# Three rounded products in place of two full-precision ones for the attended rows of the second attention block

## The reference, cut to what matters

```python
def _L1_xattn_ref(text, features, Wq, bq, Wk, bk):
    Q = jnp.einsum('btx,dx->btd', text, Wq) + bq
    K = jnp.einsum('bpx,dx->bpd', features, Wk) + bk
    scores = jnp.einsum('btd,bpd->btp', Q, K) * scale
    attn = jax.nn.softmax(scores, axis=-1)
    attended = jnp.einsum('btp,bpd->btd', attn, features)
    return attended
...
x = x + _L1_xattn_ref(_layernorm(x, axis=-1), ctx_4096, L1_xattn_Wq, L1_xattn_bq, L1_xattn_Wk, L1_xattn_bk)
```

## Time and profile before

| | |
|---|---|
| median of 3 runs | 2158.94 us (2157.11 to 2161.94) |
| the profiled execution, its own time | 2155.61 us |
| its span from the first to the last instruction | 2153.8 us |
| busy: TensorE / weight loads | 2119.5 us (98%) / 1667.0 us (77%) |
| busy: VectorE / ScalarE / GpSimd | 1854.2 us (86%) / 1155.1 us (54%) / 260.4 us (12%) |

### The profile page before, as it was taken

One profiled execution on the slowest core, in us unless ns is written; L12 is line 12 of the kernel. 1 busy time (PEld: TensorE's weight loads), 2 busy tenths in 40 slices (PEclk: granted clock), 3 DMA queues, 4 the chain that ended last, 5 costly groups with the idle time before them and its releaser, 6 DMA issues.

```text
span 2153.8 us, 35686 instructions
## 1 busy us (share of the span) xinstructions
PE 2119.5 (98%) x11487; PEld 1667.0 (77%) x11487; DVE 1854.2 (86%) x3099; ACT 1155.1 (54%) x1722; POOL 260.4 (12%) x302
## 2 busy tenths in 40 slices
PE   9979999999999999999999999999999999999998
PEld 7857777778777777787777778777777787777776
DVE  8268898988888998888898988888998888898984
ACT  4145555655555565555555655555565555555652
POOL 0001111111101110111111111101110111111100
PEclk9999999999999999999999999999999999999999
DMA  6354343333343323334343333343323334343310
GB/s 217 142 156 127 118 132 102 95 119 126 127 134 119 117 90 105 127 127 136 117 130 103 95 119 125 128 134 120 117 89 106 127 127 136 117 129 104 93 54 30
DMA packets 110874, 254.03 MB, mean 118 GB/s; under 512 B 12976, under 2 KB 14272, under 8 KB 110848
## 3 DMA queue, kind: packets, MB, share of 16 engines
q1 hardware_dynamic: 110848, 253.69, 36.3%
HBM read 215.89 MB, written 20.97 MB: 110 GB/s over the span
## 4 chain that ended last, share of the span: by engine, by line
PE 84%; DVE 6%; issue 3%; ACT 1%; DVEq 0%; POOL 0%; POOLq 0%; ACTq 0%
PE acc L1192 17%; PE shared L1121 7%; PE shared L1166 6%; PE shared L1167 6%; PE scores L1181 5%; PE scores L1180 5%; PE acc L1152 4%; PE scores L1141 4%; PE acc L1155 4%; PE acc L1153 4%; PE shared L1357 3%; PE shared L1284 3%; PE scores L1127 2%; PE scores L1307 2%; DVE neg_max L880 2%
## 5 line engine op out<-in xcount | busy, mean ns | idle before, releaser
L991 DVE TENSOR_TENSOR p_lo<-prob,p_hi 128x1024 fp32r<-128x1024 f32 x256 | 312.2, 1219 | 103.6 <-ACT p_hi L790 85.7
L783 ACT ACTIVATE prob<-scores 128x1024 f32<-128x1024 f32 x256 | 260.8, 1019 | 241.1 <-PE scores L1181 189.9
L880 DVE TENSOR_REDUCE neg_max<-scores 128x1 f32<-128x1024 f32 x256 | 309.4, 1220 | 44.8 <-PE scores L1141 42.1
L696 POOL TENSOR_TENSOR rstd<-var_eps,minus_half 128x1 f32<-128x1 f32 x128 | 126.2, 986 | 1746.1 <-DVE var_eps L870 1746.1
L790 ACT ACTIVATE p_hi<-prob 128x1024 fp32r<-128x1024 f32 x256 | 271.3, 1060 | 42.7 <-PE acc L1192 38.5
L1152 PE MATMUL acc<-m_hi,cT_hi 128*128 128x512 f32 x512 | 218.3, 426 | 3.6 <-DVE cT_lo L1052 2.7
L1166 PE MATMUL shared<-signT,y_hi 128*128 128x512 f32 x512 | 205.5, 401 | 0.0
L1155 PE MATMUL acc<-m_ring,cT_hi 128*128 128x512 f32 x512 | 203.3, 397 | 0.0
L1153 PE MATMUL acc<-m_hi,cT_lo 128*128 128x512 f32 x512 | 203.1, 397 | 0.0
L1180 PE MATMUL scores<-q_hl,k_hh 128*128 128x512 f32 x512 | 201.0, 392 | 1.8 <-DVE q_m L973 1.4
L1181 PE MATMUL scores<-q_m,k_l 128*128 128x512 f32 x512 | 202.0, 395 | 0.0
(11 more groups left out here) (219 smaller groups left out, 4201.5 us busy)
## 6 DMA issues: line engine op xcount, KB each, us to landing
m_ring<-m_low SPq DMA_DIRECT2D x512, 256.0 KB, 3.2
c_in<-in_ctx SPq DMA_DIRECT2D x32, 512.0 KB, 3.3
xn<-in_x SPq DMA_DIRECT2D x32, 512.0 KB, 4.2
x<-in_x SPq DMA_DIRECT2D x32, 512.0 KB, 3.2
c_val<-in_ctx SPq DMA_DIRECT2D x32, 512.0 KB, 3.7
out_x<-oscale SPq DMA_DIRECT2D x32, 512.0 KB, 3.0
q_m<-q_hl SPq DMA_DIRECT2D x32, 256.0 KB, 3.1
k_hh<-k_hh SPq DMA_DIRECT2D x32, 256.0 KB, 3.5
```

The lines of the kernel that those rows point to most:

```text
L783: nc.scalar.activation(prob[s % 2][:, :], scores[s % 2][:, :], ACT.Exp).then_inc(exp_ready, 1)
L880: nc.vector.tensor_reduce(neg_max[:, t:t + 1], scores[t % 2][:, :], AX_X, ALU.max, negate=True).then_inc(row_max, 1)
L991: nc.vector.tensor_tensor(p_lo[s % 2][:, :], prob[s % 2][:, :], p_hi[s % 2][:, :].bitcast(F32), ALU.subtract).then_inc(p_lo_ready, 1)
```

## The change

The context rows are split into a rounded part `val_hi` (a copy on ScalarE, after `p_hi` of step 4) and a remainder `val_lo = c_val - val_hi` (a subtraction on GpSimd, between `norm_scale(0)` and `norm_scale(3)`). The turned weights are split into `attnT_hi` (the copy on ScalarE that was `attnT`, now rounded) and `attnT_lo` (a subtraction on VectorE, behind the reciprocal of step 6). TensorE makes three products for each half instead of one. It waits for `attnT_lo` and `val_lo` ahead of the first. `val_hi` lies in the memory of `oscale`, `val_lo` in that of `c_val` and `attnT_lo` in that of `attn`.

```diff
--- before.py
+++ after.py
@@ -484,8 +484,12 @@
 
         xnT = sb("xnT", [P, T, P])
         den_wide = xnT[:, 0:2, :].rearrange("p t c -> p (t c)")
-        oscale = sb("oscale", [P, D])
-        c_val = sb("c_val", [P, D])
+        with ExitStack() as before:
+            oscale = sb("oscale", [P, D], F32, before)
+        val_hi = sb("val_hi", [P, D], F32R)
+        with ExitStack() as before:
+            c_val = sb("c_val", [P, D], F32, before)
+        val_lo = sb("val_lo", [P, D], F32R)
         stat = [sb(f"stat{i}", [P, 12]) for i in range(4)]
         mean_var = [sb(f"mean_var{i}", [P, 2]) for i in range(4)]
         neg_mean = [sb(f"neg_mean{i}", [P, 1]) for i in range(4)]
@@ -506,9 +510,11 @@
         xn_1 = xn_3 = p_sum
         xn_2 = oscale
         result = oscale
-        attn = sb("attn", [P, P])
+        with ExitStack() as before:
+            attn = sb("attn", [P, P], F32, before)
+        attnT_lo = sb("attnT_lo", [P, P], F32R)
         gate_parts = attn
-        attnT = sb("attnT", [P, P])
+        attnT_hi = sb("attnT_hi", [P, P], F32R)
         low = attn
         lowT_hi = sb("lowT_hi", [P, P], F32R)
         lowT_lo = sb("lowT_lo", [P, P], F32R)
@@ -596,6 +602,9 @@
         s_max_ready = sem("s_max_ready")
         attn_ready = sem("attn_ready")
         attnT_ready = sem("attnT_ready")
+        attnT_lo_ready = sem("attnT_lo_ready")
+        val_hi_ready = sem("val_hi_ready")
+        val_lo_ready = sem("val_lo_ready")
         x3_ready = sem("x3_ready")
         l_max_ready = sem("l_max_ready")
         l_exp_ready = sem("l_exp_ready")
@@ -707,6 +716,10 @@
                         norm_scale(2, c)
                     if prepare:
                         norm_scale(0, b)
+                    if chain:
+                        pool.wait_ge(val_hi_ready, nth(1, c, 1))
+                        pool.wait_ge(key_col_ready, nth(1, c, 1))
+                        nc.gpsimd.tensor_tensor(val_lo[:, :], c_val[:, :], val_hi[:, :].bitcast(F32), ALU.subtract).then_inc(val_lo_ready, 1)
                     if chain:
                         norm_scale(3, c)
                     if attend:
@@ -791,6 +804,10 @@
                         if chain and s == 3:
                             act.wait_ge(x2_ready, nth(2, c, 2))
                             normalize(2, c, xn_2, res)
+                        if chain and s == 4:
+                            act.wait_ge(val_loaded, nth(16, c, 16))
+                            act.wait_ge(xnT_done[2], nth(2, c, 2))
+                            nc.scalar.activation(val_hi[:, :], c_val[:, :], ACT.Identity).then_inc(val_hi_ready, 1)
                         if chain and s == 6:
 
                             act_chain.begin(c)
@@ -805,7 +822,7 @@
                         if chain and s == 6:
                             act.wait_ge(attnT_done, nth(1, c, 1))
                             act.wait_ge(att_done, nth(2, c - 1, 2))
-                            nc.scalar.activation(attnT[:, :], shared[1][:, 0:P], ACT.Identity).then_inc(attnT_ready, 1)
+                            nc.scalar.activation(attnT_hi[:, :], shared[1][:, 0:P], ACT.Identity).then_inc(attnT_ready, 1)
                     if prepare:
                         for h in range(2):
                             act.wait_ge(qk_done, nth(2, b, h + 1))
@@ -1024,6 +1041,9 @@
                         if chain and s == 6:
                             dve.wait_ge(attn_ready, nth(1, c, 1))
                             dve_chain.chain(dve, nc.vector.reciprocal(r_inv[1][:, :], r_sum[1][:, :]))
+                            dve.wait_ge(attnT_ready, nth(1, c, 1))
+                            nc.vector.tensor_tensor(attnT_lo[:, :], shared[1][:, 0:P], attnT_hi[:, :].bitcast(F32),
+                                                    ALU.subtract).then_inc(attnT_lo_ready, 1)
                     if chain:
 
                         for h in (1, 0):
@@ -1296,10 +1316,14 @@
                             transposes(0, kw, kwT_done)
                         if chain and s == 7:
                             pe.wait_ge(attnT_ready, nth(1, c, 1))
-                            pe.wait_ge(val_loaded, nth(16, c, 16))
-                            mm(shared[1][:, :], attnT[:, :], c_val[:, half(1)], start=True, stop=True).then_inc(att_done, 1)
-                            pe.wait_ge(kwT_ready, nth(2, a, 2))
-                            mm(shared[0][:, :], attnT[:, :], c_val[:, half(0)], start=True, stop=True).then_inc(att_done, 1)
+                            pe.wait_ge(attnT_lo_ready, nth(1, c, 1))
+                            pe.wait_ge(val_lo_ready, nth(1, c, 1))
+                            for h in (1, 0):
+                                if h == 0:
+                                    pe.wait_ge(kwT_ready, nth(2, a, 2))
+                                mm(shared[h][:, :], attnT_hi[:, :], val_hi[:, half(h)], start=True, stop=False)
+                                mm(shared[h][:, :], attnT_hi[:, :], val_lo[:, half(h)], start=False, stop=False)
+                                mm(shared[h][:, :], attnT_lo[:, :], val_hi[:, half(h)], start=False, stop=True).then_inc(att_done, 1)
                         if prepare and s == 7:
                             pe.wait_ge(c_loaded, nth(16, b, 16))
                             pe.wait_ge(exp_ready, nth(8, a, 7))
```

## The result

| | before | after |
|---|---|---|
| median | 2158.03 us (2154.97 to 2161.94) | 2214.05 us (2213.0 to 2214.69) |
| ratio | | 1.0256, 95% interval 1.0243 to 1.0269 |
| span of the profiled execution | 2153.8 us | 2212.8 us |

The change makes the kernel 56 us slower. A turn has become 1.83 us longer (62.14 to 63.96 us, from one start of the block's projections to the next, mean of twenty turns), and 31 times 1.83 is 56.7.

The account below looks back on a forecast made before the run. TensorE was taken to bound the whole, with VectorE without slack in the walk. Per turn 0.61 - 0.32 + 1.77 = 2.06 us, times 31 is 63.9; with 2155.6 and 3.3 that gave 2222 us, range 2178 to 2243.

Parts of the forecast that it names:

- its first rival: In the walk, GpSimd is held and VectorE keeps going; products start 2.4 us late, 2.08 a turn, 2223 us; chance 0.12.
- Sharing in pieces: GpSimd and VectorE slow each other; VectorE loses some 0.3 to 1.2 us a turn, 2177 to 2205 us; chance 0.10.
- The hold: At step 5, VectorE's p_lo waits for the end of GpSimd's val_lo: 1.77 us late, bounds 0 and 2.40.
- attnT_lo, 0.61 us late: At the attended rows, attnT_lo behind VectorE's reciprocal lets the first product start at 1097.05 instead of 1096.44: 0.61 us late.
- The saving of 0.32 us: At the attended rows, six rounded products replace two of full precision on TensorE: 0.32 us less per block.
- The sum per turn: Over one turn, late attnT_lo less TensorE's saving plus VectorE's wait: 0.61 - 0.32 + 1.77 = 2.06 us.
- val_hi free: ScalarE's copy of 1.06 us in the walk costs nothing, covered by 1.51 us of idle time, about 0.45 left.
- the fifth case: Faster: VectorE isn't held, TensorE's 0.61 us come back later in the turn, 10 us saved, 2149 us; chance 0.05.

Follow-up runs that it names:

- the run with both repairs: Changed kernel with the context rows split before the walk and attnT_lo right behind p_sum of step 6: 2156.5 us, ratio 0.9999.
- The two runs with the waits gone: Changed kernel, rows split before the walk, attnT_lo behind p_sum of step 6: 2156.5 us; the same with VectorE's den_wide copy earlier: 2157.4 us.

## Why the prediction was right

- **Slower, by 2222 us forecast and 2214 measured**, through the mechanism that it named. `p_lo` of step 5 is where the time stands, `val_lo` beside it is 2.40 us long, and TensorE idles ahead of the products of step 5, 1.24 us where some 1.4 were forecast. One sign was told wrongly: `p_lo` was to start 1.6 to 1.8 us behind `kwT`, but the profile has it start at once and last 2.77 us. What tells the forecast from its first rival is the length of `val_lo`. That rival (GpSimd is held) falls by these rows: `val_lo` keeps its length. Sharing in pieces falls by the run with half of the columns.
- **The hold, mis-sized:** 1.77 us forecast, 1.55 measured. The step was "that it then waits for the end of `val_lo`". GpSimd began 0.05 us before `shift` had ended and let go 0.13 before its own recorded end, and `p_lo` was due 0.72 after `val_lo` began instead of 0.63. The page SBUF — State Buffer of the Trainium skill, section Who interferes with whom, was borne out in the clauses that were tried: first comer keeps the way to the end, two SBUF inputs against a read, and not against a fill. The 0.13 us hardly speak against its "whole instruction": two VectorE instructions in a row also overlap by 0.09 us in the record (1.22 long, 1.13 apart). What it means by first is not the recorded start to within 0.15 us, as the split before the walk shows.
- **attnT_lo, 0.61 us late:** measured from the end of `p_lo` of step 6 to the first product, 2.23 us (1124.48 to 1126.71) against 1.62 (1094.82 to 1096.44). That is 0.61, to the digit by luck: `attnT_lo` started 0.04 us later behind the reciprocal than forecast, and the hand-over took 0.10 instead of 0.14.
- **The saving of 0.32 us:** measured from the first product to the projections, 1.46 us against 1.71, so 0.25 here; the first of the six takes 0.32 us instead of 0.23 after the wait. With no wait, in the run with both repairs, it is 0.31.
- **The sum per turn:** 1.55 + 0.61 - 0.25 = 1.91 against 1.83 measured. The missing 0.08 is given back behind the projections: from them to the product that uses the copied row sums it is 3.74 us (1128.17 to 1131.91) instead of 3.82, since TensorE comes later and no longer waits there. The forecast of 2.06 is 0.23 too high: 0.22 of it is the hold, and the smaller saving and the time given back, neither of them foreseen, nearly cancel. So do they in the run without `val_lo`, where 0.30 was measured for the forecast's 0.29.
- **val_hi free:** the exponential of step 6 starts at 1118.75, right behind the end of `p_sum` at 1118.72, as before (1090.64 and 1090.61). ScalarE's idle time ahead of it went from 1.51 to 0.57 us, so 0.57 was the cover left, not 0.45.
- **What it said of the fifth case** ("TensorE's 0.61 us are given back later in the turn") was judged rightly as unlikely, but its price was too good. It took for granted that 10 us could be had once the waits were gone. The two runs with the waits gone have none of it, while the run with the hold and the early `attnT_lo` has 0.31 us a turn: the saving was worth something only where TensorE was late.

## What to carry to other kernels

Before work is given to GpSimd, look at what VectorE does at that moment, not at GpSimd's idle time: in these runs a read of SBUF by GpSimd and a VectorE instruction with two SBUF inputs took turns, and a long one on the idle engine stopped the full one. Put it where VectorE reads PSUM or waits for its whole length, or let VectorE do it. A hold has no semaphore, so look for it as a group whose mean rose without an edit. And a saving on the busiest engine is worth its size only if the results that it meets next are early enough to be met earlier.

## What the runs showed of the hardware that was not expected

- The order of arrival decides: GpSimd, coming second, waited for one VectorE instruction and was then let in ahead of the next, although VectorE had it ready. The hold was 2.21 us.
- A recorded lead of 0.15 us did not make GpSimd first (it waited 1.26 us for the key sums), one of 0.72 did. Nothing in between was tried. The length of the held instruction doesn't matter: a one-column addition of 0.16 us was held to 2.27.
- A wait of TensorE of 2.22 us, once a turn, was followed in ten turns, about a third, by slow products, in the turns looked at with a granted clock of 0.50 for some 3 us (1.6 us on the turn). Waits of 1.24 us in the changed kernel left the turns even, 63.94 to 63.98 us.
